# Three batch-normalized edge layers: one walk instead of two in the last two, with the second moments from sums of edge rows by source

## What is computed

```
for l in range(3):
    x = jnp.concatenate([h[src], e], axis=1) @ W1[l].T + b1[l]      # (edges, 256)
    mu, var = jnp.mean(x, axis=0), jnp.var(x, axis=0)
    x = jax.nn.relu((x - mu) * rsqrt(var + 1e-5) * gamma[l] + beta[l])
    h = jax.ops.segment_sum(x @ W2[l].T + b2[l], dst)
    if l < 2:
        h = jax.nn.relu(h); e = jax.nn.relu(e)
```

## Time and profile before

| what | us |
| --- | --- |
| the three runs | 3572.55, 3563.08, 3571.81 |
| median | 3571.81 |
| span of the profiled execution | 3563.8 |
| layer 0, first walk; second walk | 522.5; 173.0 |
| layer 1, first gather to full sums | 709.2 |
| layer 2, the same | 707.1 |

### The profile page before, as it was taken

How to read it: one execution, slowest core, us unless ns; L and a number is a source line. 1 busy time by engine, 2 the same in 40 slices (tenths; PEclk the granted TensorE clock), 3 DMA queues, 4 the chain that set the end, 5 groups by cost and what they waited for, 6 DMA issues and landing times. The chain is left out here.

```text
span 3563.8 us, 57414 instructions
## 1 busy us (share of the span) xinstructions
PE 2573.6 (72%) x12616; PEld 1658.2 (47%) x12616; DVE 2008.4 (56%) x3085; ACT 1520.1 (43%) x3440; POOL 2004.8 (56%) x1999
## 2 busy tenths in 40 slices
PE   4887977767677555557996566569966655599898
PEld 1334445555555343344654344446634434356444
DVE  8886864444445444446964444459744444499211
ACT  8674343333334333334743333337633333367211
POOL 0000017777763777776847777768567777778000
PEclk7999987777768777778997777779977777799999
DMA  2002036665535788885968878849678887578200
GB/s 73 0 1 116 1 90 191 171 167 165 165 103 163 259 262 261 262 262 165 328 211 262 262 259 263 264 140 328 239 255 259 264 263 255 194 270 296 116 1 18
DMA packets 271544, 679.40 MB, mean 191 GB/s; under 512 B 48513, under 2 KB 81206, under 8 KB 270038
## 3 DMA queue, kind: packets, MB, share of 16 engines
q1 hardware_dynamic: 156758, 336.25, 28.6%
q0 software_dynamic: 73216, 190.95, 18.9%
q10 hardware_dynamic: 41472, 151.01, 11.2%
HBM read 502.07 MB, written 175.94 MB: 190 GB/s over the span
## 5 line engine op out<-in xcount | busy, mean ns | idle before, releaser
L924 PE MATMUL psum<-w_all,region 128*128 128x256 f32 x2496 | 898.0, 527 | 649.7 <-ACT region L1793 634.6
L924 PEld LDWEIGHTS psum<-w_all,region 128*128 128x128 f32 x2496 | 633.2, 265 | 914.2 <-issue 726.2
L415 POOL DMA_INDIRECT region<-tab,idx_ring x624 | 592.9, 950 | 318.7 <-issue 311.7
L415 POOL DMA_INDIRECT tN<-tab,idx_ring x624 | 590.2, 946 | 190.1 <-issue 184.0
L415 POOL DMA_INDIRECT region<-tabs,idx_ring x208 | 206.2, 991 | 577.3 <-issue 575.8
L1941 POOL TENSOR_TENSOR region<-node_no,dst_rel 128x256 f32<-128x256 f32 x312 | 409.5, 1313 | 138.1 <-ACT region L1837 116.4
L1454 DVE TENSOR_TENSOR tN<-tN,psum 128x1024 f32<-128x1024 f32 x156 | 190.5, 1221 | 433.1 <-DMA tN<-tab,idx_ring 429.0
L1446 DVE TENSOR_TENSOR acc<-acc,psum 128x1024 f32<-128x1024 f32 x312 | 379.1, 1215 | 46.2 <-ACT psum L1807 46.1
L1454 DVE TENSOR_TENSOR region<-region,psum 128x1024 f32<-128x1024 f32 x156 | 190.4, 1220 | 363.4 <-DMA region<-tab,idx_ring 342.0
L1807 ACT ACTIVATE psum<-region 128x1024 f32<-128x1024 f32 x156 | 160.2, 1027 | 448.8 <-DVE acc L1446 297.8
L1807 ACT ACTIVATE psum<-tN 128x1024 f32<-128x1024 f32 x156 | 160.2, 1027 | 407.6 <-DVE acc L1446 407.6
(11 more groups left out here) (308 smaller groups left out, 3482.4 us busy)
## 6 DMA issues: line engine op xcount, KB each, us to landing
region<-e_t SPq DMA_DIRECT2D x416, 256.0 KB
pre_dram<-region ACTq DMA_DIRECT2D x144, 512.0 KB, 3.7
pre_dram<-tN ACTq DMA_DIRECT2D x144, 512.0 KB, 4.0
region<-pre_dram SPq DMA_DIRECT2D x144, 512.0 KB, 5.0
tN<-pre_dram SPq DMA_DIRECT2D x144, 512.0 KB, 5.0
tA<-dst_row SPq DMA_DIRECT2D x78, 256.0 KB
adj_kept<-region SPq DMA_DIRECT2D x5, 2000.0 KB, 16.9
region<-adj_kept SPq DMA_DIRECT2D x5, 2000.0 KB, 17.2
```

The lines of the kernel that those rows point to most:

```text
L415: pool.indirect_dma_start(m_ring[j][:, c, at:at + width], None, table[:, :], bass.IndirectOffsetOnAxis(ap=idx_at(j, k)[:, c:c + 1], axis=0 ...
L924: mm = pe.matmul(banks[:, 2 * (j % 2) + c // 2, (c % 2) * 256:(c % 2) * 256 + 256], e_ring[:, j % E_SLOTS, c * D:(c + 1) * D], W(f"ee{l}") ...
```

## The change

**Layers 1 and 2 walk once** (`merged_pass`). Their statistics are ready before the walk: the sum of p from the outdegrees as before; the sum of squares as the outdegrees times the squared table, plus twice the products of the table with the ReLU'd edge attributes summed by source node (`src_sums`), plus a 128x128 matrix of the attributes' products (`gram`) with the weights. In the walk a group is gathered, added to, cut off at `low` and summed into its window, with the one-hots made by VectorE (`dve_one_hot`). Nothing is stored to or read from `pre_dram`, and no squares are made.

**Layer 0 keeps two walks**, and its first has 130 units beside its 104 groups, 10 per trip (1, 1, 1, 2, 1, 1, 1, 2). A unit is 512 edge rows of one source tile, read from `by_tile` (270 KB). VectorE makes a row mask and one-hots of the source's place in its tile, ScalarE four masked ReLUs of 128x128, TensorE 4 matmuls of 256 columns that give the sums by source and the products, and VectorE adds the two into `tA` and `gram`. Behind the walk ScalarE sums `tA`, TensorE turns its 25 tiles, and ScalarE copies them to `src_sums`.

**by_tile** is written once. In the setup VectorE finds each edge's place (25 masks, 25 running sums, 25 predicated copies, 416 elements per partition each). SyncE loads the edge rows in pairs of chunks (135 KB) to a ring of 4, and GpSimd writes each chunk with an indirect DMA (`put_rows`): 208 before it reads `irregular`, 144 behind that, 64 between block 1's gathers and layer 0's. The pool of descriptors for such DMAs is halved (`dynamic_dma_scratch_size=8192`). Some semaphores have other names and `pre_in`, `pre_out` are `from_dram`, `to_dram`.

```
+ROW = D + 4
+STAGES = 4
+PAIRS = NG * GC // 2
+PUT_ENDS = (0, 104, 176, PAIRS)
...
+UNITS_AT = [range(10 * j // UNROLL, 10 * (j + 1) // UNROLL) for j in range(UNROLL)]
+UNITS = 10 * TRIPS
+assert UNITS >= (EP + N_TILES * (GE - 1)) // GE
+TABLE = UNITS + 2
+U_ROWS = 5
...
+        m_again = m_ring[0:4] + [tA[:, k * GC * 2 * D:(k + 1) * GC * 2 * D].rearrange("p (c f) -> p c f", c=GC) for k in range(3)
+                                 ] + [tN[:, 0:GC, :]]
...
+            for t in range(N_TILES):
+                last = dve.tensor_scalar(masks[:, t, :], tile_of, float(t), 0.0, ALU.is_equal, ALU.add,
+                                         accum_out=tile_cnt[:, t:t + 1])
+            last.then_inc(S["setup_to_pe"], 1)
...
+            ran, chosen = [], []
+            for t in range(N_TILES + 1):
+                if t > 1:
+                    dve.wait_ge(v.sem, chosen[t - 2])
+                if t < N_TILES:
+                    ran.append(v.did(dve.tensor_tensor_scan(acc_ps[:, t % 2, 0:NG * GC], ones[:, 0:1].to_broadcast([D, NG * GC]),
+                                                            masks[:, t, :], tile_base[:, t:t + 1], ALU.mult, ALU.add)))
+                if t:
+                    dve.wait_ge(v.sem, ran[t - 1])
+                    chosen.append(v.did(dve.copy_predicated(place_f, masks[:, t - 1, :].bitcast(U16),
+                                                            acc_ps[:, (t - 1) % 2, 0:NG * GC])))
+            dve.wait_ge(v.sem, chosen[-1])
+            dve.tensor_scalar(place[:, :], place_f, -1.0, None, ALU.add).then_inc(S["tile_tables"], 1)
...
+            def source_unit(u, m):
+                pe.wait_ge(S["u_made"], 2 * u + 2)
+                pe.nop(nofuse=True)
+                pe.wait_ge(S["u_relu"], u + 1)
+                pe.nop(nofuse=True)
+                pe.wait_ge(S["u_add"], T["u_add"] + u - 1)
+                for c in range(GC):
+                    mm = pe.matmul(unit_ps(m), u_both[:, m % 2, c, D:2 * D], u_both[:, m % 2, c, :], start=(c == 0),
+                                   stop=(c == GC - 1))
+                mm.then_inc(S["u_mm"], 1)
...
+                pe.wait_ge(S["stat_in"], T["stat_in"] + 1)
+                with pe.Fori(0, TRIPS) as i:
+                    edge2(l, i, 0)
+                    for j in range(UNROLL):
+                        if j + 1 < UNROLL:
+                            edge2(l, i, j + 1)
+                        for m in UNITS_AT[j]:
+                            source_unit(i * 10 + m, m)
...
+            def merged_pass(l):
+                for t in range(N_TILES):
+                    pe.matmul(st_ps[0:1, 0:2 * D], outdeg[:, t:t + 1], tN[:, t, :], start=(t == 0), stop=False)
+                pe.matmul(st_ps[0:1, 0:2 * D], src_total[:, :], W(f"ee{l}"), start=False, stop=True)
+                for t in range(N_TILES):
+                    pe.matmul(acc_ps[:, 0, 0:2 * D], src_sums[:, t, :], tN[:, t, :], start=(t == 0), stop=False)
+                pe.matmul(acc_ps[:, 0, 0:2 * D], gram, W(f"ee{l}"), start=False, stop=True).then_inc(S["st_mm"], 1)
+                for n, (lo, hi) in enumerate(SQ_PARTS):
+                    pe.wait_ge(S["sq"], T["sq"] + n + 1)
+                    for t in range(lo, hi):
+                        mm = pe.matmul(st_ps[0:1, 2 * D:4 * D], outdeg[:, t:t + 1], squares[:, t, :], start=(t == 0),
+                                       stop=(t == N_TILES - 1))
...
+                def scatter2(i, j):
+                    g = i * UNROLL + j
+                    pe.wait_ge(S["msg"], T["msg"] + g + 1)
+                    pe_wide(pe, T, wide, g, [(lambda c, j=j: m_again[j][:, c, 0:D], D),
+                                             (lambda c, j=j: m_again[j][:, c, D:2 * D], D)])
+                    pe_window(pe, T, g, j, 2, m_again)
+                    pe_turn_window(pe, T, g, (j + 1) % 2, 2, merged_ps)
...
+                with pe.Fori(0, TRIPS - 1) as i:
+                    for j in range(UNROLL):
+                        edge2(l, i, j + 1)
+                        scatter2(i, j)
...
+            def unit_prepare(u, i, m):
+                dve.wait_ge(S[f"from_dram{m % U_ROWS}"], T[f"from_dram{m % U_ROWS}"] + 16 * ((10 // U_ROWS) * i + m // U_ROWS + 1))
+                dve.nop(nofuse=True)
+                dve.wait_ge(S["u_mm"], T["u_mm"] + u - 1)
+                rows = u_rows[:, m % U_ROWS, :, :]
+                dve.tensor_scalar(u_mask[:, m % 2, :], row_no[:, :], unit_left[:, bass.ds(u, 1)], None, ALU.is_lt)
+                dve.tensor_scalar(u_lane[:, m % 2, :].unsqueeze(2), rows[:, :, D:D + 1].bitcast(I32), D - 1, None,
+                                  ALU.bitwise_and).then_inc(S["u_made"], 1)
+                dve.wait_ge(S["u_made"], 2 * u + 1)
+                dve.tensor_tensor(u_both[:, m % 2, :, 0:D], node_no[:, :].unsqueeze(1).to_broadcast([D, GC, D]),
+                                  u_lane[:, m % 2, :].unsqueeze(2).to_broadcast([D, GC, D]), ALU.is_equal).then_inc(S["u_made"], 1)
+
+            def unit_add(u, m):
+                at = dve.value_load(unit_i[0:1, bass.ds(u + TABLE, 1)], min_val=0, max_val=NP - D)
+                to, of = tA[:, bass.ds(at, D)], unit_ps(m)
+                dve.wait_ge(S["u_mm"], T["u_mm"] + u + 1)
+                dve.wait_ge(S["u_add"], T["u_add"] + u)
+                dve.tensor_tensor(to, to, of[:, 0:D], ALU.add)
+                dve.tensor_tensor(gram, gram, of[:, D:2 * D], ALU.add).then_inc(S["u_add"], 1)
...
+                        if j:
+                            add_squares(g - 1, j - 1)
+                        for m in UNITS_AT[j]:
+                            unit_prepare(i * 10 + m + 1, i, m + 1)
+                            unit_add(i * 10 + m, m)
...
+            def merged_pass(l, bet):
+                dve.wait_ge(S["st_mm"], T["st_mm"] + 1)
+                dve.tensor_tensor(low_diag, acc_ps[:, 0, 0:2 * D], W(f"ee{l}"), ALU.mult).then_inc(S["stat_in"], 1)
+                dve.wait_ge(S["st_mm"], T["st_mm"] + 2)
+                v.did(dve.memset(a0, 0.0))
+                count_tables(T)
+                turned_shift(l, statistics(bet, merged_ps, a1))
+                with dve.Fori(0, TRIPS) as i:
+                    for j in range(UNROLL):
+                        g = i * UNROLL + j
+                        dve.wait_ge(S[f"rows_in{j}"], T[f"rows_in{j}"] + 16 * GC * (i + 1))
+                        dve.wait_ge(S["ve_mm"], T["ve_mm"] + g + 1)
+                        p = m_again[j].rearrange("p c f -> p (c f)")
+                        dve.tensor_tensor(p, p, edge_ps(j), ALU.add).then_inc(S["pre"], 1)
+                        w0 = dve_window_start(dve, g - LAG)
+                        dve_wide(dve, T, wide, g, sums2)
+                        dve_one_hot(dve, T, g, j)
+                        dve.wait_ge(S["pre"], T["pre"] + g + 1)
+                        dve.tensor_tensor(m_again[j], m_again[j], low[:, :].unsqueeze(1).to_broadcast([D, GC, 2 * D]), ALU.max
+                                          ).then_inc(S["msg"], 1)
+                        dve_window(dve, T, g, w0, (j + LAG) % 2, 2, merged_ps)
...
+                    for c in range(GC):
+                        r = act.activation(u_both[:, m % 2, c, D:2 * D], u_rows[:, m % U_ROWS, c, 0:D], ACT.Relu,
+                                           scale=u_mask[:, m % 2, c:c + 1])
+                    r.then_inc(S["u_relu"], 1)
...
+                for n, (lo, hi) in enumerate(SQ_PARTS):
+                    act.activation(squares[:, lo:hi, :], tN[:, lo:hi, :], ACT.Square).then_inc(S["sq"], 1)
...
+            def put_rows(lo, hi):
+                for q in range(lo, hi):
+                    k = q % STAGES
+                    pool.wait_ge(S[f"from_dram{k}"], 16 * (q // STAGES + 1))
+                    for c in range(2):
+                        pool.indirect_dma_start(by_tile[:, :], bass.IndirectOffsetOnAxis(ap=place[:, 2 * q + c:2 * q + c + 1], axis=0),
+                                                stage[:, k, c, :], None).then_inc(S[f"put{k}"], 16)
+
+            put_rows(*PUT_ENDS[0:2])
...
+            put_rows(*PUT_ENDS[1:3])
...
+            put_rows(*PUT_ENDS[2:4])
...
+            def merged_pass(l):
+                with pool.Fori(0, TRIPS) as i:
+                    for j in range(UNROLL):
+                        g = i * UNROLL + j
+                        pool_idx(pool, T, i, j)
+                        if j == UNROLL - 1:
+                            pool.wait_ge(S["st_mm"], T["st_mm"] + 1)
+                            pool.nop(nofuse=True)
+                            pool.wait_ge(S["sq"], T["sq"] + 1)
+                            pool.nop(nofuse=True)
+                        pool.wait_ge(S["sc_mm"], T["sc_mm"] + g - (UNROLL - 1))
+                        pool.nop(nofuse=True)
+                        pool_gather(pool, j, 0, tab2, 0, 2 * D, "rows_in", m_again)
...
+            def load_unit(u, m):
```

(19 more changed lines are left out.)

530 lines of the change are left out of this document (387 added, 143 removed).

## The result

The changed kernel takes 3541.28 us (median of 3538.78 to 3544.06) beside 3570.2 for the kernel before: a ratio of 0.9927, 95% interval 0.9913 to 0.9941. The forecast was 3461; the change has the sign forecast and a quarter of the size, 29 us instead of 111. The profiled execution's span is 3540.2 us, 23.6 under that of before.

The account below looks back on a forecast made before the run. VectorE bounds the counting, GpSimd's gathers the first walks, TensorE the second walks. Terms 55 + 1 + 0 + 28.5 + 91 + 9.5 - 296 = -111; 3563.8 - 111 = 3452.8, + 8.0 = 3461 us; range 3335 to 3560 (forecast's own 3400 to 3520).

Parts of the forecast that it names:

- What bounds the kernel: Stage by stage: VectorE in the counting, GpSimd's gathers in first walks (5.0 us per group), TensorE in second walks.
- The lock: Layers 1 and 2's one walk: gathers lose 0.25 us per group to VectorE's two-input operations, giving 5.25 per group, 546 us.
- The rival with the lock: Layers 1 and 2: each gather waits out each two-SBUF-input VectorE operation; 6.65 us per group, 3753 us in all; chance 0.05.
- The start of the one-walk layers: Ahead of layers 1 and 2's walk: about 44.5 us of statistics, hidden by seven or eight groups of gathers but for 3.
- Second lot: 144 writes to by_tile, 180 us, between the counts' check and block 1's first gather: 0 us, until a put costs 1.34.
- Third lot: Last 64 writes to by_tile, between block 1's last gather and layer 0's first: +28.5 us, bounds 20 and 45.
- Setup: New VectorE masks, running sums and predicated copies ahead of the counting: +55 us, from 47 to 62.
- Layer 0's walk: Layer 0's first walk with 130 units: 5.9 us per group, 614 us instead of 522.5, +91; bounds 572 and 697.
- The bound by TensorE's clock: Layer 0's first walk: clock staying at half, products 8.1 us per group, 3690 us; decides from 7.0 per group; chance 0.07.
- Layer 0's end: Behind layer 0's first walk: transposes of the sums with copies 6.5 us, plus statistics and last unit: +9.5 us.

Follow-up runs that it names:

- disturbed sets: Four of the seven sets of runs, where the kernel before took 4397 to 4436 us; the changed kernel there took 4762 us, ratio 1.0816.

## Why the prediction was wrong

- **What bounds the kernel** was right: layers 1 and 2 are GpSimd's, and every microsecond that a gather loses there is lost.
- **The lock** is the step that failed: "I take 0.25: 5.25 per group". It took the tenth that block 1 pays of its 1.69 us of two-input operations and carried it, raised to 0.25 us, to operations of another length. Measured was 0.53, 0.28 more for 96 groups, 27 us per layer. The price isn't a share of the time. A gather must start inside the operation, and then waits for the rest of it. My estimate from these rows: where gathers come every 1.25 us and their starts fall evenly, an operation of length d costs about (d - 0.13) squared / 2.5. The 0.13 is what a plain gather's 0.945 us is longer than the 0.82. That gives 0.48 for 1.22 us (measured 0.49), 0.04 for the one-hot (0.04), 0.09 to 0.14 for four pieces of 0.36 to 0.43 (0.10), and 0.125 + 0.02 + 0.035 = 0.18 for block 1, which paid 0.16. All of it stood in the trace of before: 3.50 beside 3.43 was the same law, not a case against block 1. The rival with the lock had the mechanism and, at 1.65 us per group, three times the price, since it let every gather wait for every operation.
- The Trainium skill's exclusive lock, under which the other engine fully blocks (page SBUF — State Buffer, section Who interferes with whom), agrees with the traces for a gather that starts inside an operation with two inputs in SBUF. The same section infers that a `tensor_tensor` leaves the generation of descriptors alone; these indirect gathers waited for it (1.62, 1.84 and 3.50 us), and the measurement decides. A gather that already runs isn't held up, and the add with an input in PSUM holds up none: 99 gathers started inside it, and the only 3 long ones started in its last moments, when the one-hot had begun.
- **The start of the one-walk layers**: 3 us of stall forecast, 12.7 measured in layer 1 and 11.5 in layer 2. The statistics were timed rightly and the wrong wait was looked at; the indexes' copy behind the fourth group's add was in the diff, at `hand_on`. That is 9 to 10 us per layer, less 2 for the first eight groups, which ran at 5.0 and not 5.25. With the lock's 27 it makes some 34 in each layer, where 36 and 33 are missing.
- **Second lot, "0, until a put costs 1.34"**: a write took 1.26, as forecast, and it still cost 22. The slack of 12 us left out that the lot can't start with the check, its rows' load being behind the spills (19 us), and that block 1's table stores stand behind all its loads in SyncE's queue (the first of them 17 us ahead of the first gather).
- **Third lot** +34.3 against 28.5: by the step as told, SyncE's loads ended at 1207.7, 76 us behind the last gather where I had 70 and 2.8 to the last load.
- **Setup** +59.8 to the check against 56: 56.8 ahead of the counting where I had 55, and 3.0 in it where I had 1. Two sizes in the first term cancel: the running sum is near the upper bound of 1.18, and the masks came every 0.51 us where I had 0.60. The Trainium skill's half throughput (page DVE: opcode table, instruction layouts, handler registers and perf-mode slots, section 6) agrees, 1.093 against 0.59. The term of about 60 that I worked out by it would have been 3 too high.
- **Layer 0's walk** was right to 5 us, in part by luck. I had full clock give 5.55 and added the rest for stretches at half; the clock was 0.96. The double steps cost more than forecast, and so does a trip's end, which I didn't count. The bound by TensorE's clock was not met.
- **Layer 0's end**, +9.5 against +5.8: the 25 transposes took 5.3 us where I had 6.5 with their copies, and the second walk's first three maxima ran beside them.

## What to carry to other kernels

Price a lock between two engines by how often the second one starts inside an operation of the first, times what is then left: it goes with the square of the operation's length, so cut a long one in pieces (73 us here; in the disturbed sets it brought nothing), or give it an input in PSUM (for the maximum, not tried). When a walk is moved onto a queue's idle time, look through what is queued behind it on the engine that feeds it, not only for idle time on the engine that does it.

## What the runs showed of the hardware

An indirect write of 128 rows of 528 bytes costs GpSimd what a gather does, 0.96 us and 0.30 of issue. A gather that starts inside a VectorE operation with two inputs in SBUF ends 0.82 us after that operation (1.62, 1.84 and 3.50 us in all, where its own 0.95 isn't longer), one that already runs takes its 0.95, and the operation isn't lengthened. Gathers lose nothing to VectorE's adds that read PSUM. And the same kernel before ran at 3570 us in some sets and at about 4400 in others, on one chip in both ways (3566 and 4436), with a change that gains 0.7% in the one and loses 8% in the other.
